# Four expert tiles of the first MoE layer, listed from ten sequences, run between the two stages

## What is computed

```python
x = x + _L0_xattn_ref(_layernorm(x, axis=-1), ctx_1024)   # causal K K^T applied to Q
x = x + _L0_ffn_ref(_layernorm(x, axis=-1), ...)          # attention of 16 heads, then 8 experts of width 512, top 2
x = x + _L1_xattn_ref(_layernorm(x, axis=-1), ctx_1024, ...)  # cross attention, 16 heads of 64
x = x + _L1_ffn_ref(_layernorm(x, axis=-1), ...)          # 16 experts of width 256, top 2, and a shared expert
```

```python
vals, idx = jax.lax.top_k(probs, K)
...
hid = jax.nn.silu(jnp.einsum('td,edf->tef', t, w1)) * jnp.einsum('td,edf->tef', t, w3)
y_e = jnp.einsum('tef,efd->ted', hid, w2)
y = jnp.einsum('ted,te->td', y_e, gate)
return res + y.reshape(b, s, D)
```

## Time and profile before

| | |
|---|---|
| runs of the kernel before | 918.62 us median of 3 (918.09 to 921.11) |
| the profiled execution | 916.48 us, span 914.6 us |
| PE busy / DVE / ACT / POOL | 854.8 (93%) / 709.8 (78%) / 607.7 (66%) / 278.1 (30%) us |
| mean granted TensorE clock | 0.992 of 2.4 GHz |

### The profile page before, as it was taken

How to read it: one execution, slowest core, us unless ns; L and a number is a source line. 1 busy time by engine, 2 the same in 40 slices (tenths; PEclk the granted TensorE clock), 3 DMA queues, 4 the chain that set the end, 5 groups by cost and what they waited for, 6 DMA issues and landing times.

```text
span 914.6 us, 23436 instructions
## 1 busy us (share of the span) xinstructions
PE 854.8 (93%) x7788; PEld 766.7 (84%) x7788; DVE 709.8 (78%) x1976; ACT 607.7 (66%) x1719; POOL 278.1 (30%) x359
## 2 busy tenths in 40 slices
PE   4799989758999999998899999999999999999997
PEld 3677656528999999997799988899889989999996
DVE  4888888766897666676988888877688548888867
ACT  4488889945666666675777776777775327777740
POOL 3865577660000000005432333411223003333320
PEclk9999999988999999999999999999999999999999
DMA  8236700022111411103100121210044942333335
GB/s 313 80 131 257 310 24 25 31 88 93 53 59 59 151 48 48 52 24 133 35 25 25 59 83 47 82 60 25 24 169 167 389 92 89 103 97 96 105 118 195
DMA packets 43032, 92.92 MB, mean 102 GB/s; under 512 B 6081, under 2 KB 29505, under 8 KB 41505
## 3 DMA queue, kind: packets, MB, share of 16 engines
q1 hardware_dynamic: 36048, 72.61, 22.9%
q0 software_dynamic: 6864, 18.80, 6.1%
HBM read 62.22 MB, written 29.17 MB: 100 GB/s over the span
## 4 chain that ended last, share of the span: by engine, by line
PE 65%; DVE 8%; issue 2%; DMA 2%; ACT 1%; POOL 1%; ACTq 0%; DVEq 0%; POOLq 0%
PE ps L982 17%; PE ps L788 11%; PE ps L789 11%; PE ps L790 11%; PE ps L1075 3%; PE ps L1099 3%; PE ps L1085 3%; PE ps L1157 2%; DMA BIG<-ys_dram,YI 2%; DVE BIGR L1903 1%; PE ps L954 1%; PE ps L955 1%; DVE X L1938 1%; PE ps L944 1%; ACT BIGR L1304 0%
## 5 line engine op out<-in xcount | busy, mean ns | idle before, releaser
L788 PE MATMUL ps<-BIGR 128*128 128x256 f32 (+1 forms) x970 | 298.4, 308 | 9.0 <-DVE BIGR L1903 3.9
L790 PE MATMUL ps<-BIGR 128*128 128x256 f32 (+1 forms) x922 | 262.7, 285 | 0.0
L789 PE MATMUL ps<-BIGR 128*128 128x256 f32 (+1 forms) x746 | 218.6, 293 | 0.0
L788 PEld LDWEIGHTS ps<-BIGR 128*128 128x128 f32 x970 | 185.4, 191 | 18.4 <-issue 14.2
L982 PE MATMUL ps<-BIG 128*128 128x128 f32 x1424 | 180.5, 275 | 0.0
L790 PEld LDWEIGHTS ps<-BIGR 128*128 128x128 f32 x922 | 175.9, 191 | 0.7
L982 PEld LDWEIGHTS ps<-BIG 128*128 128x128 f32 x1424 | 169.9, 192 | 0.1
L789 PEld LDWEIGHTS ps<-BIGR 128*128 128x128 f32 x746 | 143.3, 192 | 1.9
L2146 POOL DMA_INDIRECT BIG<-ys_dram,YI x32 | 34.4, 1076 | 222.0 <-DMA ys_dram<-BIG 213.9
L1443 ACT ACTIVATE BIG<-ps,BIG 128x128 f32<-128x128 f32 x256 | 91.4, 384 | 15.4 <-DVE BIG L1983 15.2
L2132 POOL DMA_INDIRECT xs_dram<-TT,PI x64 | 65.9, 1030 | 73.1 <-ACT PI L1284 58.4
(11 more groups left out here) (264 smaller groups left out, 1857.2 us busy)
## 6 DMA issues: line engine op xcount, KB each, us to landing
BIG<-in_wgu SPq DMA_DIRECT2D x2, 6144.0 KB, 19.3
BIG<-in_wd SPq DMA_DIRECT2D x2, 4096.0 KB, 22.6
BIG<-xs_dram SPq DMA_DIRECT2D x47, 129.5 KB, 2.1
BIG<-xs_dram SPq DMA_DIRECT2D x39, 128.0 KB, 2.0
ys_dram<-BIG SPq DMA_DIRECT2D x39, 128.0 KB, 1.7
BIG<-in_wkv SPq DMA_DIRECT2D x2, 2048.0 KB, 9.8
kv_dram<-BIG SPq DMA_DIRECT2D x16, 256.0 KB, 2.1
BIG<-in_wgu SPq DMA_DIRECT2D x2, 2048.0 KB, 9.8
```

The lines of the kernel that those rows point to most:

```text
L788: pe.matmul(o, l[0], r[0], start=start, stop=False)
L789: pe.matmul(o, l[0], r[1], start=False, stop=False)
L790: return pe.matmul(o, l[1], r[0], start=False, stop=stop)
```

## The change

Four tiles (AHEAD = 4) are taken out of the first expert stage and run before it. After ten sequences (COUNTED = 10) a new DVE phase `a_route` counts how many full tiles each expert has, takes the first four and writes their experts and rows to `AI`. PE loads the four experts' numbers into registers (`a_reg`); SP loads the rows (`a_xs`); PE transposes them (`a_xT`) and multiplies in plain fp32 with the tokens as the stationary side and 512 (gate, up) or 256 (down) weight columns moving from WGU and WD at the register's address. ACT evicts (`a_xT_e`), applies silu (`a_silu`), copies (`a_hT_e`, `a_y`), DVE multiplies (`a_hm`), SP stores the results behind the others in `YS` (`a_ys`). The tiles' buffers lie in the context array CT, part of which SP loads again afterwards (`ct_back`, 1.25 MB). The list of the expert stage starts behind these rows (`behind`), so NT0 is 35 and PAIRED 14; `places` sends tokens of the four tiles to their results. The 30 fillers go (FILL = (0, 24)). The table LEAD is new throughout, and so is the order in all stages.

```diff
+AHEAD = 4
+COUNTED = 10
...
-NT0 = 32 + E0 - 1
+NT0 = 32 + E0 - 1 - AHEAD
...
-PAIRED = 2 * -(-(2 * NB * 128 - E0 * 255) // 256)
+PAIRED = 2 * -(-(2 * NB * 128 - 128 * AHEAD - E0 * 255) // 256)
...
-FILL = (30, 24)
+FILL = (0, 24)
+AHEAD_ROWS = (8, 9, 10, 11, 6, 7)[:AHEAD]
...
-    "EC": -100, "EL": -200, "ET": -100, "ET_e": 300, "K": -300, "K_e": 100, "NT": -400, "PV": -300, "Q_e": -200,
...
+    "a_route": 247, "a_xs": -1137, "a_reg": -84, "a_xT": -19, "a_xT_e": 33, "a_gate0": -16, "a_gate1": -12590,
...
+def ahead_phases(p):
+    p.add("DVE", 2200, ("a_route",), ("rb", 0, COUNTED - 1), due=AHEAD_DUE)
+    for i in range(AHEAD):
...
+        add("SP", 700, "a_xs", ("a_route",), ("sc", 0, COUNTED - 1), ("ctx", COUNTED - 1), ("load_w0b",), late=2200)
+        add("PE", 600, "a_reg", ("a_route",), ("load_w0b",))
+        add("PE", 220, "a_xT", ("a_xs", i), ("s", NB - 1), banks=["a_xT_e"])
+        add("ACT", 310, "a_xT_e", ("a_xT", i), ("a_up1", i - 2))
+        add("PE", 860, "a_gate0", ("a_xT_e", i), ("a_reg", i), banks=["a_silu"])
...
+        add("ACT", 470, "a_silu", ("a_gate1", i), ("a_hT", i - 2))
+        add("DVE", 600, "a_hm", ("a_up1", i), ("a_silu", i))
+        add("PE", 450, "a_hT", ("a_hm", i), banks=["a_hT_e"])
+        add("ACT", 490, "a_hT_e", ("a_hT", i), ("a_down1", i - 2), *[("ctx", b) for b in (13,) if i % 2])
...
+            def a_reg(i):
+                if i == 0:
+                    pe.wait_ge(sem("ahead_listed"), 1)
...
+                expert[i] = pe.value_load(AI[i:i + 1, 0:1], min_val=0, max_val=E0 - 1)
...
+            def a_gate_up(i, which, k):
...
+                at = k * 2 * F0 + (F0 if which == "up" else 0)
+                m = pe.matmul(ps(*key)[:, :], AXT[i % 2][:, k * 128:k * 128 + 128],
+                              WGU[:, bass.ds(expert[i] * (4 * F0) + at, F0)], start=k == 0, stop=k == 1)
...
+            def a_hT(i):
+                vacant(pe, "a_hT", i)
+                pe.wait_ge(*emptied("a_up0", i))
+                for c in range(4):
+                    at = slice(c * 128, c * 128 + 128)
+                    m = pe.transpose(ps("a_hT", i)[:, at], AH[i % 2][:, at], ident)
...
+                for c in (2 * x, 2 * x + 1):
+                    m = pe.matmul(ps(*key)[:, 0:D], AHT[i % 2][:, c * 128:c * 128 + 128],
+                                  WD[:, bass.ds(expert[i] * (2 * F0) + c * D, D)], start=c == 0, stop=c == 3)
...
+            def a_xT_e(i):
...
+                    m = act.mul(AXT[i % 2][:, at], ps("a_xT", i)[:, at], g2c[:, k:k + 1])
...
+                act.activation(AH[i % 2], ps("a_gate0", i)[:, :], ACT.Silu).then_inc(*frees("a_gate0", i))
...
+            def a_hm(i):
+                v.wait_ge(*full("a_up0", i))
+                v.wait_ge(*emptied("a_gate0", i))
+                v.tensor_tensor(AH[i % 2], ps("a_up0", i)[:, :], AH[i % 2], ALU.mult).then_inc(*frees("a_up0", i))
...
+                for i, t in enumerate((ahead_row, behind)):
+                    v.tensor_tensor(OHw, oh, t.rearrange("p (o n) -> p o n", o=1).broadcast_to([128, 2 * NB, E]),
+                                    ALU.mult).then_inc(dv, next_step("dve"))
+                    then()
+                    v.tensor_reduce(RP[:, 32 * i:32 * i + 32], OHw, AX, ALU.add).then_inc(dv, next_step("dve"))
...
+            def a_xs(i):
+                if i == 0:
+                    sp.wait_ge(sem("ahead_listed"), 1)
...
+                    for n in range(3):
+                        sp.wait_ge(sem(f"scattered{n}"), 32 * len(range(n, COUNTED, 3)))
+                at = sp.value_load(AI[i:i + 1, 1:2], min_val=0, max_val=E0 * CAP - 128)
...
+            def ct_back():
+                sp.wait_ge(sem("ahead_stored"), 16 * AHEAD)
+                for lo, hi in ((0, 8), (10, 12)):
+                    sp.dma_start(CT[:, lo:hi, :, :], a["ctxT"][:, lo:hi, :, :]).then_inc(sem("ct_loaded2"), 16)
```

More of the change, by code:

```diff
@@ L281, in latent_phases, with add @@
     p.add("DVE", 400, ("gates_b", 0), ("gates_e", 0))
+def ahead_phases(p):
+    p.add("DVE", 2200, ("a_route",), ("rb", 0, COUNTED - 1), due=AHEAD_DUE)
+    for i in range(AHEAD):
+        def add(engine, ns, name, *after, banks=(), **kw):
+            p.add(engine, ns, (name, i), *after, banks=[("s", (q, i)) for q in banks], due=AHEAD_DUE + 20 * i, **kw)
+        add("SP", 700, "a_xs", ("a_route",), ("sc", 0, COUNTED - 1), ("ctx", COUNTED - 1), ("load_w0b",), late=2200)
[3 more added lines that the diff above has]
+        add("PE", 860, "a_gate0", ("a_xT_e", i), ("a_reg", i), banks=["a_silu"])
+        add("PE", 860, "a_gate1", ("a_gate0", i))
+        add("PE", 860, "a_up0", ("a_gate1", i), banks=["a_hm"])
+        add("PE", 860, "a_up1", ("a_up0", i))
+        add("ACT", 470, "a_silu", ("a_gate1", i), ("a_hT", i - 2))
+        add("DVE", 600, "a_hm", ("a_up1", i), ("a_silu", i))
+        add("PE", 450, "a_hT", ("a_hm", i), banks=["a_hT_e"])
+        add("ACT", 490, "a_hT_e", ("a_hT", i), ("a_down1", i - 2), *[("ctx", b) for b in (13,) if i % 2])
+        add("PE", 860, "a_down0", ("a_hT_e", i), banks=["a_y"])
+        add("PE", 860, "a_down1", ("a_down0", i))
+        add("ACT", 330, "a_y", ("a_down1", i))
+        add("SP", 60, "a_ys", ("a_y", i), late=2000)
+    p.add("SP", 100, ("ct_back",), ("a_ys", AHEAD - 1), ("down", 0, 4), late=8000)
 def expert_phases(p, r, start):
@@ L379, in cross_phases @@
         for b in (2 * j, 2 * j + 1):
-            add("POOL", 2550, ("ga", 0, b), ("ys", 0, NT0 - 1), ("places",), ("pro1", b - 2),
+            add("POOL", 2550, ("ga", 0, b), ("ys", 0, NT0 - 1), ("a_ys", AHEAD - 1), ("places",), ("pro1", b - 2),
                 late=4000 if b < 2 else 2800)
@@ L734, in program @@
         SC1 = float(HD1 ** -0.5)
+        ct_ = CT[:, :, :, :].rearrange("p b k t -> p (b k t)")
+        AXS = [ct_[:, b * D:b * D + D] for b in AHEAD_ROWS]
+        AXT = [btg[:, :], small1[:, 0:D]]
+        AH = [ct_[:, b * D:b * D + F0] for b in (2, 4)]
+        AHT = [ct_[:, b * D:b * D + F0] for b in (0, 12)]
+        behind, ahead_row = AE[:, 0:E0], AE[:, E0:2 * E0]
         iota, ecap = (cst["iota0"], cst["iota1"]), (cst["ecap0"], cst["ecap1"])
@@ new lines, in a_gate_up @@
+            def a_gate_up(i, which, k):
+                key = f"a_{which}0", i
+                if k == 0:
+                    vacant(pe, *key)
+                    if which == "gate":
+                        pe.wait_ge(*emptied("a_xT", i))
+                at = k * 2 * F0 + (F0 if which == "up" else 0)
+                m = pe.matmul(ps(*key)[:, :], AXT[i % 2][:, k * 128:k * 128 + 128],
+                              WGU[:, bass.ds(expert[i] * (4 * F0) + at, F0)], start=k == 0, stop=k == 1)
+                if k == 1:
+                    m.then_inc(*fills(*key))
@@ L1163, in tensor @@
+            for phase, *at in ORDER["PE"]:
+                if phase in ("a_gate0", "a_gate1", "a_up0", "a_up1"):
+                    a_gate_up(at[0], phase[2:-1], int(phase[-1]))
+                elif phase in ("a_down0", "a_down1"):
+                    a_down(at[0], int(phase[-1]))
+                elif phase in ("pT0", "pT1", "pT2", "pT3"):
                     pT(at[0], int(phase[2]))
@@ L1168, in tensor @@
                 else:
-                    {"kv": kv, "ctx": ctx, "q1": q1, "hnT": hnT, "foldT": foldT, "fold": fold, "qkv": qkv, "qkT": qkT, "s": s, "pv": pv, "wup": up,
+                    {"a_reg": a_reg, "a_xT": a_xT, "a_hT": a_hT, "kv": kv, "ctx": ctx, "q1": q1, "hnT": hnT, "foldT": foldT, "fold": fold, "qkv": qkv, "qkT": qkT, "s": s, "pv": pv, "wup": up,
                      "cnt": cnt, "xT": xT, "down": down, "K": K, "V": V, "Q": Q, "S": scores, "T": T,
@@ L1174, in rows_before @@
         def rows_before(r, j):
[L1176 removed]
+            return len(range(j % 3, AHEAD, 3)) + (len(range(j % 3, NT0, 3)) if r else 0) + j // 3
         def stores_before(r, j):
@@ L1372, in kv_e, with a_silu, a_hT_e, a_y @@
                 act.copy(kvs_[m % 4], ps("kv", m)[:, :]).then_inc(*frees("kv", m))
+            def a_xT_e(i):
+                act.wait_ge(*full("a_xT", i))
+                if i >= 2:
+                    act.wait_ge(*full("a_up0", i - 2))
+                for k in range(2):
+                    at = slice(k * 128, k * 128 + 128)
+                    m = act.mul(AXT[i % 2][:, at], ps("a_xT", i)[:, at], g2c[:, k:k + 1])
+                    if k:
+                        m.then_inc(*frees("a_xT", i))
+            def a_silu(i):
+                act.wait_ge(*full("a_gate0", i))
+                if i >= 2:
+                    act.wait_ge(*full("a_hT", i - 2))
+                act.activation(AH[i % 2], ps("a_gate0", i)[:, :], ACT.Silu).then_inc(*frees("a_gate0", i))
+            def a_hT_e(i):
+                act.wait_ge(*full("a_hT", i))
+                if i >= 2:
+                    act.wait_ge(*full("a_down0", i - 2))
+                if i == 1:
+                    act.wait_ge(*full("ctx", 13))
```

(10 more changed lines are left out.)

113 lines of the change are left out of this document (97 added, 16 removed), and 26 rows, old and new, of the table LEAD.

## The result

The changed kernel takes 921.82 us (median of 12 runs, 917.34 to 923.93), the kernel before 917.88 in the same comparison: ratio 1.0039, 95% interval 1.0025 to 1.0053. It is slower by 0.4%; the forecast was 910.7, and its range ended at 918. The profiled execution took 922.98 us, with a span of 921.2 against 914.6; these two executions lie 6.6 us apart, the medians 3.9.

The account below looks back on a forecast made before the run. ACT was taken to bound the latent stage and PE's products the expert stage. Eight terms (-18.2 + 3.3 + 4.9 - 2.2 + 2.3 + 0.5 + 1.5, and 0) sum to -7.9 off the 918.62 median: 910.7 us, range 902.5 to 918.

Parts of the forecast that it names:

- step 8: Moves, transfers and the new order of the later stages: 0 us, bounds -3 and +3.
- 1: Expert stage: four tiles leave it, 4.55 us of PE each, -18.2 us.
- 2: The same tiles' plain fp32 work elsewhere on PE: about 3.3 us stand behind the first gate, +3.3 us.
- 4: Start of the expert stage: some 24 products run at full clock instead of the low level, -2.2 us.
- 7: `places` on DVE in the expert stage grows to 7.4 us in one piece: +1.5 us, bounds 0 and 2.7.
- 3: Passage from latent to expert stage: a longer chain brings the first gate at 214.1, +4.9 us, bounds 2.5 and 7.
- 5: `a_route` on DVE ahead of sequence 12's maxima takes 3.2 us, delaying ACT: +2.3 us, bounds 0 and 3.2.
- 6: Register loads and addresses by register on PE, 0.63 us issue time per load: +0.5 us, bounds 0 and 4.
- A: Passage tail hidden: PE time alone decides, `a_route` and `places` cost nothing; -14.6, so 904 us; chance 0.2.
- B: Rows for `a_xT(0)` come late from sequence 9's scatter, delaying PE: about +6, so 917 us; chance 0.12.
- C: Passage: waits drop PE's clock, ahead work runs at 1.2 GHz; +13.5 + 2.2, so 926 us; chance 0.08.

Follow-up runs that it names:

- with the pieces: The changed kernel with its 6 MB weight load cut into six of 1 MB, each issued behind one more sequence's token write: 909.78 us, ratio 0.9931 to the kernel before.

## Why the prediction was wrong

**The step that failed is step 8**: "The new order of the later stages swaps steps on engines with slack. 0". I priced the order at nothing nearly everywhere but in the passage, and gave bounds of 3 us "from the few us that PE idles in all of them". For the later stages that held (+2.2). For the latent stage ahead of the passage the sum had `a_route` and the register loads but no term for the new order at all, a zero without a reason, and there it cost 10.4; of the chances only 0.05 was left for new waits, and only in the later stages. A bound from idle time that is there says nothing of idle time that a new order makes. The trace of before held the warning: a row with a wait of 0.38 us for a scatter that had taken 14.8. Such a wait is a slack of nothing, on ACT, the engine that I had named as the bound of the stage, and the instruction order showed `tt(5)` earlier, `sc(2)` later and a weight load later.

**The other steps.**
- *1, 2, 4 and 7, the expert stage:* -14.5 measured, -15.6 forecast. The first products run 0.12 us apart (228.35, 228.47 below), so term 4 came in full. `places` was mis-sized: PE's stall behind it is 3.47 us where it was 0.60, so +2.9 and not +1.5, just past the bound of 2.7. The piece grew from 4.8 us to 7.6 on DVE, and all of that growth came through: its cover was used up before.
- *3, the passage:* +2.9, not +4.9; up to `pv(15)` it is 0.8 longer, as forecast. The chain is the one described: the load of the table, the silu, `a_hm(0)`, then `onrm(15)`. From `pv(15)` to `cnt(15)` it takes 8.3 us instead of 5.6, where I had 3.6 more; and from `cnt(15)` to the gate it is 0.5 shorter, where I had 0.5 longer.
- *5, `a_route`:* +4.7 in the changed kernel, +3.5 with the pieces, not +2.3. It takes 4.3 us of DVE, not 3.2; ACT waited 2.61 us behind it and PE behind ACT, and the clock fell (0.83 in 160 to 180; 0.91 with the pieces).
- *6, the register loads:* 0.63 us each was right. The stretch from the scores of 13 to 15, where two of them stand, grew by 1.5 us (0.8 with the pieces), not 0.5; how much of that is the loads', no run shows.

PE's rows of the changed kernel in the passage and behind, which answer to the earlier trace rows (`a_xT(0)`, `wup(14)`, `pv(15)`, `a_hT(0)`, `wup(15)`, `cnt(15)`, `gate(0,0)`), and the stall behind `places`:

```profile
198.45 0.33 PE L1214 MATMUL ps<-CS,CT 128*128 128x128 f32 x1 [0.80 <-ACT BIG L1342]
...
200.04 0.67 PE L971 MATMUL ps<-small,BIG 128*128 128x264 f32 x2
...
205.63 1.08 PE L962 MATMUL ps<-BIG 128*32 128x128 f32 x32
...
208.70 0.63 PE L1234 MATMUL ps<-CS,CT 128*128 128x128 f32 x4 [1.99 <-DVE CT L1915]
...
210.88 0.61 PE L971 MATMUL ps<-small,BIG 128*128 128x264 f32 x2
...
213.91 0.17 PE L979 MATMUL ps<-mb,strictb 128*128 128x8 bf16 x1
...
228.16 0.35 PE L829 MATMUL ps<-BIGR 128*128 128x256 f32 x1
228.35 0.28 PE L830 MATMUL ps<-BIGR 128*128 128x256 f32 x1
228.47 0.28 PE L831 MATMUL ps<-BIGR 128*128 128x256 f32 x1
...
268.35 0.35 PE L829 MATMUL ps<-BIGR 128*128 128x256 f32 x1 [3.47 <-DVE BIGR L2043]
```

The stall behind `places` in the kernel before:

```profile
249.96 0.36 PE L788 MATMUL ps<-BIGR 128*128 128x256 f32 x1 [0.60 <-DVE BIGR L1903]
```

DVE's and ACT's rows of the changed kernel: the first and last row of `a_route` and the maximum behind it, and the exponentials that waited for that maximum:

```profile
165.52 0.16 DVE L1880 TENSOR_TENSOR sc<-CNT,CS 128x8 f32<-128x8 f32 x1
...
169.56 0.22 DVE L1910 TENSOR_SCALAR AE<-AE 128x8 f32<-128x8 f32 x1
169.63 0.68 DVE L1701 TENSOR_REDUCE BIG<-ps 128x4 f32<-128x512 f32 x1
```

```profile
170.35 2.17 ACT L1342 ACTIVATE BIG<-ps,BIG 128x128 f32<-128x128 f32 x8 [2.61 <-DVE BIG L1701]
```

**The rivals.** A (all hidden) fell: the first gate is 2.9 us later from the last scores, and `a_route` and `places` cost. B (late rows) fell: `a_xs` is issued at 195.30 and `a_xT(0)` starts at 198.45 behind a wait for ACT, not for a DMA. C had the right sign and the wrong place. PE's clock did fall, to 0.83 to 0.88 in the stretches around the hole and behind `a_route`, but in the passage it stayed at 1.00 (200 to 220), and the ahead products ran at full speed. The Trainium skill (TensorE: Matmul & The Clock Gate, section HAM oscillation), whose kernel falls to the low level at each wait between its groups of products, fits the two places where PE was mostly idle for some microseconds (9.54 us ahead of 120.24; waits of 0.90, 1.47 and 0.63 us shortly ahead of 173.92). In the passage, for which I had weighed it, this execution shows no fall. For the table the Trainium skill (ScalarE: Activation LUTs, section What ACT_TABLE_LOAD costs) adds a drain of 1.38 us to the load. Here the load began 0.02 us after the row ahead of it, and the silu 0.02 us after the load's end, so the trace disagrees, and the load alone is the price:

```profile
205.65 0.20 ACT L1375 CAST PI<-PF 128x2 int32<-128x2 f32 x1
205.87 1.28 ACT L1480 ACT_TABLE_LOAD   x1
207.17 0.60 ACT L1480 ACTIVATE CT<-ps 128x512 f32<-128x512 f32 x1
```

With the hole away, the changed kernel stands at 909.8, close to the 910.7 of the sum. In the profile of that kernel the first gate comes 7.4 us later than before and all behind it is 15.2 us shorter; the sum had 7.7 and 15.6. That agreement is partly luck: it hides errors that cancel, `a_route` and `places` dearer, the passage cheaper.

## What to carry to other kernels

A table of offsets that is new throughout is a change of every stage, and each stage wants a price. Look in the trace of before for waits across queues that show a few tenths only, above all those on a transfer that took several times its median: they sit at the edge, and here 5 us of shift on either side (the waiting instruction, the issue of the scatter) came through in full. A long weight load that is issued 100 us before its first product (96.27 and 200.72 here) can be issued in pieces, each behind a small transfer that someone waits for: worth 1.1% in the changed kernel by the ratios, and nothing in the kernel before, whose wait was 0.38 us.

## What the runs showed of the hardware

- A scatter of 128 rows that lands in 2.6 us (median) landed 11 to 16 us after its second issue while 6 to 8 MB of weights streamed at some 400 GB/s. With a single piece of 1 MB beside it (issued at 103.16, the next only behind `tt(5)`) it was through by 111.48, at most 5.5 us after its issue at 105.97.
- A load of a register on PE shows as 0.63 us of issue time, the same as on ACT.
- The same order of instructions got a granted clock of 0.91 in one kernel's execution and 1.00 in another's over the same 20 us, behind the same wait of PE of 1.99 us.
